# A graph network kernel on one core: a tail of unused gathers on POOL and single-row DMAs on SP and ScalarE

## The reference

```python
edge_in = node_feats[src] * edge_feats[:, None]
msg = jax.nn.relu(edge_in @ W_msg + b_msg)
agg = jax.ops.segment_sum(msg, dst, num_segments=N)
x = _layernorm(x + relu(agg @ W_out + b_out))
...
def _rgcn_layer(x, W, SW, b, src, dst, rel):
    xt = jnp.einsum('nd,rde->rne', x, W)
    agg = jax.ops.segment_sum(xt[rel, src], dst, num_segments=N)
    return jax.nn.relu(agg + x @ SW + b)
...
x = _layernorm(x + _rgcn_layer(_rgcn_layer(x, ...), ...))
```

## Time and profile before

| | us |
|---|---|
| device time, median of 2 runs | 7510.7 |
| lowest and highest run | 7509.95, 7511.46 |
| span of the profiled execution, first to last instruction | 6622.7 |
| median of the runs less the span | 888.0 |
| POOL busy in the span | 4948.3 (75%) |
| TensorE matmul busy | 3199.1 (48%) |

### The profile page before, as it was taken

The page is one execution under the profiler, slowest core; times in us unless marked ns, Lnnn a source line. Parts: engine busy times, 40 slices in busy tenths (PEclk is TensorE's granted clock), DMA queues, the critical chain, the costliest instruction groups (busy, mean ns, idle before and its releaser), DMA issues. The chain is left out here.

```text
span 6622.7 us, 52372 instructions
## 1 busy us (share of the span) xinstructions
PE 3199.1 (48%) x12124; PEld 2491.7 (38%) x12124; DVE 1746.3 (26%) x4136; ACT 686.1 (10%) x2063; POOL 4948.3 (75%) x5004
## 2 busy tenths in 40 slices
PE   4455555555555444444445544443444444443443
PEld 4344444444444333333333333333333333333333
DVE  3344444444444311111111111111111111111112
ACT  1112222222222100000000000000000000000000
POOL 4777777777777677777777777767777777777776
PEclk7566666656666656666665666665555555555555
DMA  4122222222222222222222222221222222222222
GB/s 130 52 80 83 83 83 83 83 83 83 83 83 87 76 54 76 76 75 75 75 72 76 76 75 76 76 77 50 56 57 58 58 58 57 57 57 56 58 57 55
DMA packets 255517, 474.23 MB, mean 72 GB/s; under 512 B 90635, under 2 KB 143412, under 8 KB 255454
## 3 DMA queue, kind: packets, MB, share of 16 engines
q0 software_dynamic: 159744, 327.48, 19.1%
q1 hardware_dynamic: 92620, 144.65, 6.0%
q10 hardware_dynamic: 3090, 1.38, 0.1%
HBM read 351.16 MB, written 121.98 MB: 71 GB/s over the span
## 5 line engine op out<-in xcount | busy, mean ns | idle before, releaser
L576 POOL DMA_INDIRECT rows<-rel_table,index x3328 | 3306.4, 994 | 1070.0 <-issue 1009.7
L622 PE MATMUL bank<-onehot,rows 128*128 128x128 f32 x9984 | 2337.4, 408 | 3369.7 <-DMA rows<-rel_table,index 2340.9
L622 PEld LDWEIGHTS bank<-onehot,rows 128*128 128x128 f32 x9984 | 2024.6, 301 | 3668.2 <-DMA rows<-rel_table,index 1590.4
L576 POOL DMA_INDIRECT rows<-msg_table,index x1664 | 1629.8, 979 | 587.6 <-issue 583.3
L608 DVE TENSOR_TENSOR agg<-agg,bank 128x128 f32 x624 | 179.5, 288 | 3569.0 <-PE bank L622 3540.5
L596 DVE SCALAR_TENSOR_TENSOR rows<-rows,weight,bm 128x128 f32<-128x128 f32 x1664 | 474.6, 347 | 1146.8 <-DMA rows<-msg_table,index 1146.8
L584 DVE TENSOR_TENSOR onehot<-columns,place 128x1024 f32<-128x1024 f32 x624 | 765.8, 1227 | 19.6 <-issue 9.7
L819 PE MATMUL bank<-wr,feat 128*128 128x512 f32 x784 | 641.8, 969 | 3.5 <-ACT feat L767 2.4
L568 ACT ACTIVATE rows<-rows 128x512 f32<-128x512 f32 x416 | 261.8, 629 | 1657.9 <-DVE rows L596 1657.9
L819 PEld LDWEIGHTS bank<-wr,feat 128*128 128x128 f32 x784 | 236.9, 332 | 198.8 <-issue 194.6
L559 ACT ACTIVATE index<-rel_index 128x8 int32 (+1 forms) x416 | 85.4, 207 | 1546.4 <-DMA rows<-rel_table,index 1542.3
(11 more groups left out here) (65 smaller groups left out, 628.6 us busy)
## 6 DMA issues: line engine op xcount, KB each, us to landing
rel_table<-tab SPq DMA_DIRECT2D x196, 512.0 KB, 2.7
rows<-rel_table,index POOLq DMA_INDIRECT x3328, 2.5
rows<-msg_table,index POOLq DMA_INDIRECT x1664, 2.5
x_dram<-normed SPq DMA_DIRECT2D x98, 64.0 KB, 2.9
xin<-x_dram SPq DMA_DIRECT2D x98, 64.0 KB, 2.0
xin<-in_x_dram SPq DMA_DIRECT2D x97, 64.0 KB, 2.4
out_dram<-normed SPq DMA_DIRECT2D x97, 64.0 KB, 2.0
tab<-in_x_dram SPq DMA_DIRECT2D x24, 256.0 KB, 2.8
```

The costliest lines, as they stand in the source:

```text
L576: nc.gpsimd.indirect_dma_start(rows[:, st.u, t, :], None, table, bass.IndirectOffsetOnAxis(ap=index[:, st.u, t:t + 1], axis=0)).then_inc(s ...
L622: ins = nc.tensor.matmul(ps_edge[k][:, 0:P], rows[:, st.u, t, :], onehot[:, k, t, :], start=t == 0, stop=t == TPG - 1)
```

## The change

After the last group of layer 2, POOL gets 81 further gathers (`pool_spare`) from `rel_tables[0]` into a new SBUF tensor `spare` that nothing reads, in 14 batches. Eleven batches of six gather 128, 127, 126, 125, 124, 120, 112, 96, 64, 32 and 16 rows of 512 B. Then come six gathers of 128 rows with a bounds check in the DMA, three of 128 rows of 1024 B, and six of 128 rows of 256 B. Batch n uses the half `n % 2` of `spare` and waits for batch n - 2 to have landed. After the last, POOL waits for all and releases SP.

SP, behind its waits for all stores, loads six row indices from `rel_index` into registers and issues six DMAs of one row of 512 B at those addresses, four times over (`row_spare`), waits for the 24 rows, and releases ScalarE. ScalarE does the same with 24 rows. Only then does the closing barrier of all engines come.

```diff
--- before.py
+++ after.py
@@ -184,6 +184,7 @@
         slot = sb("slot", [P, 1], I32)
         slot_f = sb("slot_f", [P, 1])
         quad = sb("quad", [P, 4])
+        spare = sb("spare", [P, 2, 6, D])
 
         bank = [ctx.enter_context(nc.psum_tensor(f"bank{i}", [P, 512], F32)) for i in range(8)]
         ps_tab = [bank[0], bank[1]]
@@ -250,6 +251,10 @@
         s_pool_turn = sem("s_pool_turn")
         s_dve_turn = sem("s_dve_turn")
         s_zero = sem("s_zero")
+        s_spare = [sem(f"s_spare{h}") for h in range(2)]
+        s_spare_pool = sem("s_spare_pool")
+        s_spare_sp = sem("s_spare_sp")
+        s_spare_row = [sem(f"s_spare_row{h}") for h in range(2)]
 
         class EdgeSems:
             def __init__(self, name):
@@ -954,6 +959,62 @@
                     if eng is not nc.gpsimd:
                         node_loop(eng, layer)
 
+        PARTS_OF = (128, 127, 126, 125, 124, 120, 112, 96, 64, 32, 16)
+        SPARE = 6
+
+        def pool_spare(eng):
+            eng.wait_ge(lay.te, BATCHES * IN_ORDER)
+            n = 0
+            for m in PARTS_OF:
+                need(eng, s_spare[n % 2], 16 * SPARE * (n // 2))
+                pass_waits(eng, s_pool_turn)
+                for t in range(SPARE):
+                    eng.indirect_dma_start(
+                        spare[0:m, n % 2, t, :], None, rel_tables[0],
+                        bass.IndirectOffsetOnAxis(ap=rel_index[0:m, n, t:t + 1], axis=0)
+                    ).then_inc(s_spare[n % 2], 16)
+                n += 1
+            need(eng, s_spare[n % 2], 16 * SPARE * (n // 2))
+            pass_waits(eng, s_pool_turn)
+            for t in range(SPARE):
+                eng.indirect_dma_start(
+                    spare[:, n % 2, t, :], None, rel_tables[0],
+                    bass.IndirectOffsetOnAxis(ap=rel_index[:, n, t:t + 1], axis=0),
+                    bounds_check=NP * R - 1, oob_is_err=False
+                ).then_inc(s_spare[n % 2], 16)
+            n += 1
+            need(eng, s_spare[n % 2], 16 * SPARE * (n // 2))
+            pass_waits(eng, s_pool_turn)
+            pairs = rel_tables[0].rearrange("(n k) d -> n (k d)", k=2)
+            for t in range(0, SPARE, 2):
+                eng.indirect_dma_start(
+                    spare[:, n % 2, t:t + 2, :].rearrange("p t d -> p (t d)"), None, pairs,
+                    bass.IndirectOffsetOnAxis(ap=msg_index[:, n, t:t + 1], axis=0)
+                ).then_inc(s_spare[n % 2], 32)
+            n += 1
+            need(eng, s_spare[n % 2], 16 * SPARE * (n // 2))
+            pass_waits(eng, s_pool_turn)
+            halves = rel_tables[0].rearrange("n (k d) -> (n k) d", k=2)
+            for t in range(SPARE):
+                eng.indirect_dma_start(
+                    spare[:, n % 2, t, 0:D // 2], None, halves,
+                    bass.IndirectOffsetOnAxis(ap=rel_index[:, n, t:t + 1], axis=0)
+                ).then_inc(s_spare[n % 2], 16)
+            n += 1
+            for h in range(2):
+                eng.wait_ge(s_spare[h], 16 * SPARE * ((n + 1 - h) // 2))
+            eng.sem_inc(s_spare_pool, 1)
+
+        def row_spare(eng, h):
+            for p in range(4):
+                _, at = nc.values_load_multi_w_load_instructions(
+                    rel_index[p:p + 1, 0, :], engines=[eng.engine], min_val=0, max_val=NP * R - 1,
+                    skip_runtime_bounds_check_because="the DMA checks its address")
+                for t in range(6):
+                    eng.dma_start(spare[p:p + 1, h, t, :], rel_tables[0][bass.ds(at[t], 1), :]
+                                  ).then_inc(s_spare_row[h], 16)
+            eng.wait_ge(s_spare_row[h], 16 * 24)
+
         def window_check(eng):
 
             eng.wait_ge(lay.flag, 1)
@@ -982,6 +1043,9 @@
             layers(eng, unfit)
             for ring in (node_sems[0].tst, node_sems[0].nst, node_sems[1].tst, node_sems[2].nst):
                 all_stored(eng, ring)
+            eng.wait_ge(s_spare_pool, 1)
+            row_spare(eng, 0)
+            eng.sem_inc(s_spare_sp, 1)
 
         @block.gpsimd
         def _(eng):
@@ -1004,6 +1068,7 @@
             with eng.If(unfit != 0):
                 pool_sort()
             layers(eng, unfit)
+            pool_spare(eng)
 
         @block.vector
         def _(eng):
@@ -1044,6 +1109,8 @@
             message_table(eng)
             eng.wait_ge(s_w, WEIGHTS)
             layers(eng, unfit)
+            eng.wait_ge(s_spare_sp, 1)
+            row_spare(eng, 1)
 
 
 # ---- launch: one core; inputs and output as the reference has them ----
```

## The result

The changed kernel takes 7638.7 us (median of 2 runs, 7626.3 and 7651.0) against 7510.7: a ratio of 1.017, 95% interval 1.0145 to 1.0195. The forecast was 7632.

A forecast was written before the change was run, and what follows sets the result against it. POOL's stream of gathers was taken to set the time; POOL's 81.6 us past the old end, SP's 18.3 and ScalarE's 21.0 with the barrier make 120.9, on 7510.7 giving 7631.6 us, range 7603 to 7698.

The forecast's parts named there:

- The verdict and the size: Whole kernel: 120.9 us more, 1.6%, so within 2%; chances same 0.69, slower 0.30, faster 0.01.
- The chain POOL, SP, ScalarE, one behind the other: Tail: each engine starts after the one before, and only 16.9 us can run beside the old end.
- POOL's part: The 81 tail gathers at 1.25 us each, less 7.5: 81.6 us past the old end.
- If the busy 0.95 us go by the gather ... by the row ... I take the middle, 7.5 us off: POOL's small gathers: no saving if work goes by the gather, 15.0 us if by the row; 7.5 taken.
- Rival 1: POOL, 30 gathers not a multiple of 16 rows: slow step of 2.23 us, 29.4 more, 157.8 in all; chance 0.22.
- Rival 2: 127-row gathers: one DMA engine carries each, batch 3 starts 13.8 us later, 134.7 in all; chance 0.13.
- Rival 3: Tail: POOL's work by the row, 7.5 us off, rows at 0.30 us, 15 off; 98.4 in all; chance 0.06.
- my 0.57 and 0.66: Single-row DMAs: us per row with register addresses, 0.57 on SP and 0.66 on ScalarE.
- Landing and the two row parts: Behind POOL's last gather: landing 4.55 us and release 0.2, SP's rows 18.3, ScalarE's with the barrier 21.0.
- Rival 4: Rows on SP and ScalarE: each single-row DMA pays its round trip, 115 us more, 236 in all; chance 0.04.
- Taking what lies outside the span as unchanged: Device time: the 888.0 us above the span of 6622.7 were carried over unchanged to the forecast.
- The cover: Old end: 16.9 us from the last old gather's issue to the end, all that can hide a POOL tail.

The follow-up runs named there:

- experiment 5: The changed kernel again, no edit, on another chip with late signals: 7638.0 against 7504.4 us, ratio 1.0171.
- experiment 2: The changed kernel with the rows of SP and ScalarE taken out, POOL's 81 gathers kept: 6814.8 against the unchanged kernel's 6708.9 us, ratio 1.0162.
- experiment 3: The changed kernel with POOL's gathers taken out, the 48 row DMAs kept: 6739.2 against the unchanged kernel's 6708.9 us, ratio 1.0052.
- experiment 4: The changed kernel with gather sizes 128, 122, 123, 121, 119, 113, 96, 62, 31, 17, 13: 6846.1 us, ratio 1.0211 to the unchanged kernel.
- experiment 1: The unchanged kernel again, no edit, on a chip without late signals: 6709.9 us, span 6708.2.
- experiment 10: The unchanged kernel again, no edit, on a chip with late signals: 7503.5 us, span 7501.7.
- experiment 12: The changed kernel with ScalarE copying row indices three groups ahead instead of two: 7535.5 against the unchanged kernel's 7544.9 us, ratio 0.9983.
- experiment 6: The changed kernel with sizes 113, 62, 16, 128, 127 in pairs, then 120, every second batch with the bounds check: 7666.1 us.
- experiment 7: The changed kernel with one register loaded ahead of each row DMA, instead of six ahead of six: 7666.8 us (one run).
- experiment 8: The unchanged kernel with ScalarE copying row indices three groups ahead instead of two: 7370.8 against 7505.9 us, ratio 0.9828.
- experiment 9: The unchanged kernel with four of each group's eight matmuls left out: 7400.7 us, ratio 0.9863.
- experiment 11: The unchanged kernel with six of each group's eight matmuls left out: 7346.5 against 7544.9 us, ratio 0.9743.

## Why the prediction was right, and where it was not

**The verdict and the size: right.** Forecast 120.9 us more, measured 128, and 133.6 on the second chip (experiment 5), 137.2 with other sizes. The chain POOL, SP, ScalarE, one behind the other, is shown by experiments 2, 3 and 5: the parts measured alone cost 105.9 and 30.2 us, 136.1 together (some 5 of them the closing that only experiment 2 shows), and 133.6 in one kernel. But that the sum came so near is partly luck: POOL's part was 19.7 us dearer than forecast, and the landing and the rows 11.9 us cheaper where SP's first issues were short (7.0 where they weren't).

**"If the busy 0.95 us go by the gather ... by the row ... I take the middle, 7.5 us off": wrong, and this is the term that was mis-sized.** It is neither. POOL's busy time for a gather is 0.84 us and 0.0134 for each of m / k rows, m the row count and k its largest divisor up to 16 (experiment 4: ten sizes within 0.02 us; of the sizes not used to set it, 126, 124 and 120 rows come out up to 0.03 dearer). Measured batch by batch in experiment 2's trace, against six steps of 1.25: the batch of 127 rows costs 9.6 us more, 124 rows 2.0, 125 rows 1.5, 126 and 120 rows 0.2 each, the checked batch 0.4. The small sizes save 1.7 us together and not 7.5. 19.7 us in all, and POOL's issues took 112.2 us where I had 92.5.

**Rival 1, odd sizes made slower:** half right. The dearer ones are dearer because they divide badly, not because they are odd: 121 and 119 rows cost 1.0 and 1.08 us, 31 rows 1.26. My price of 29.4 us for 30 gathers was 13.5 in fact, 0.45 a gather where 0.73 would have decided, and so the kernel stayed under 2%. On a chip where the base is 6709 us, 134 to 137 us are right at 2% (experiment 4: 1.0211, 1.0193 to 1.0230).

**Rival 2, one DMA engine for a whole gather:** the split that it draws from the Trainium skill, DMA: Bandwidth & Descriptors, "Why a DMA increments its semaphore by 16 and not by 1", is what the busy times follow; the trace agrees (127 rows 2.57 us, 126 rows 0.98, 125 rows 1.19). But it was priced on the wrong engine. I let the DMA engine be late and POOL go on at its step. In the trace POOL itself needs 2.54 us for a gather of 127 rows. The data keeps up with that: in experiment 2 the six land 8.0, 7.7, 7.5, 7.6, 7.6 and 7.4 us after their start, with no queue building up, and before the batch of 125 rows there is no gap (0.30 us idle). Which DMA engines carried the rows isn't seen, neither the split of one gather nor whether the six took one engine or six; only POOL's time follows the divisor.

**Rival 3, cheaper than it looks:** wrong on POOL, since its work doesn't go by the row, and part right on the rows: their steps were 0.41 and 0.38 us, between its 0.30 and my 0.57 and 0.66.

**Landing and the two row parts:** 4.75 us from the last gather's start to SP's first instruction was 2.5. The last four old gathers took 3.4 to 4.6 us to land and those of 128 rows in the tail mostly 2.4 to 2.5 (experiment 2), near the median of 2.5 that the earlier trace rows had. Why the last four of a program take longer, no run shows. SP's 18.3 us were 14.6 (experiments 3 and 4) and 19.4 where the first issues took 0.70 us; ScalarE's 21.0 were 15.1. An issue step with register addresses of one row is 0.41 us on SP and 0.38 on ScalarE (0.23 of it the issue), not 0.57 and 0.66, and a load of six registers 0.78 and 0.83, not 0.46. Rival 4, a round trip for each row, is refuted. These errors are 2.3, 3.7 and 5.9 us, 11.9 in sum. SP's step of 0.57 came from a loop in which `load_sheet` has a semaphore wait between the two issues, and ScalarE's 0.66 took 0.16 over from it.

**"Taking what lies outside the span as unchanged": a wrong step that did no harm.** The device time is the span and 1.7 to 1.8 us (experiments 1 and 10). The profile before is an execution without late TensorE signals: no add of its layers 1 and 2 starts over 0.6 us behind the recorded end of its matmuls. The two runs of 7510 us were most likely executions with them, since that is the time of experiment 10's chip; they have no trace of their own. That the sum survived was luck: the tail doesn't use TensorE and is as long in both kinds. From the last old gather to the end it takes 151.2, 150.5 and 151.0 us with late signals (the first trace after, experiments 5 and 12). Without them it takes 154.4 in experiment 4; less the 8.8 us for its sizes and with the 4.9 us of SP's slow first issues that is 150.5. The cover can differ: 16.9 us by the earlier trace rows, 12.9 of it to the last store's issue, where experiment 5 has 29.0 to it.

## What to carry to other kernels

Work out what a tail costs on the engine that issues it, gather by gather, and cut gathers into row counts with a large divisor up to 16: 96 rows are cheaper than 31. Compare the span with the device time before an estimate rests on either, and where they don't agree, ask whether both are of the same kind of execution before giving the rest a place. And an engine that is three groups ahead instead of two was worth 1.7% on a chip with late signals; look for the next link of the chain before more lead is given to one, since here the waits for the four row buffers took up 211 of the 504 us. More buffers weren't tried.

## What the runs showed of the hardware that I had not expected

- POOL's busy time for a gather of m = 13 to 128 rows of 512 B is 0.84 us and 0.0134 for each of m / k rows, k the largest divisor of m up to 16, with 0.30 us between two gathers. At 128 rows it is 0.94 to 0.96 us at 256, 512 and 1024 B a row, so the width costs nothing here. The bounds check adds 0.04 to 0.05 us at 16, 62, 113, 127 and 128 rows.
- A load of one register takes 0.46 to 0.50 us by the median, one of six 0.78 on SP and 0.83 on ScalarE (the first on ScalarE 0.58). On ScalarE the DMA issue behind a load takes 0.46 to 0.52 us instead of 0.23.
- In the changed kernel's first trace and on the three chips of experiments 5 to 7, 8 to 10, and 11 and 12, TensorE's results come up to 34 to 40 us after the recorded ends of its matmuls, over 12 us late in 33 to 42% of a layer's groups of the unchanged kernel (experiment 10), which takes about 7500 us there. In the profile before (span 6622.7) and on the chip of experiments 1 to 4 (6709 us) there is no such lateness; the 86 us between these two are POOL's busy time (4948.3 and 5034.6). Recorded ends are modelled, so they don't show the lateness; the reader sees it in the engine behind, as waits for "remote". With fewer matmuls a group's late step is shorter (27, 22 and 10.5 us in experiments 10, 9 and 11), which speaks for a TensorE that works slowly and against a signal held back for a fixed time, and doesn't settle it. The granted clock is 0.53 in such waits (layers 1 and 2 of experiment 10), and 0.50 in all of layer 2 on the chip without them. What makes a chip do this, and what ends a stretch, stays open.
- SP's first issues of the tail took 0.70 us in four traces (the first one after, experiments 5, 7 and 12) and 0.23 to 0.31 in three others (experiments 3, 4 and 6); experiments 5 to 7 ran on one chip. The cause is open; it is worth 5 us.
